# Two extra f16 products per group of heads in the causal self-attention of a three-layer kernel

## The reference, cut to what matters

```python
def _L0_attn_ref(x, Wq, bq, Wk, bk, Wv, bv, Wo, bo):
    B, S, E = x.shape                      # 4, 128, 1024
    H = 16; D = E // H                     # 16 heads of 64
    q, k, v = ...                          # three projections, rope on q and k
    scores = jnp.einsum('bshd,bthd->bhst', q, k) / jnp.sqrt(jnp.asarray(D, x.dtype))
    scores = jnp.where(causal[None, None], -jnp.inf, scores)
    attn = jax.nn.softmax(scores, axis=-1)
    out = jnp.einsum('bhst,bthd->bshd', attn, v).reshape(B, S, E)
    return out @ Wo + bo
```

## Time and profile before

| | us |
|---|---|
| median of 3 runs (lowest to highest) | 2761.11 (2759.78 to 2761.98) |
| the profiled execution, its own time | 2763.46 |
| its span, first to last instruction | 2761.6 |
| TensorE busy in the span | 2529.8 (92%) |
| VectorE / ScalarE / GpSimd busy | 2068.7 (75%) / 1142.1 (41%) / 859.8 (31%) |
| mean granted TensorE clock | 0.964 of 2.4 GHz |

### The profile page before, as it was taken

One profiled execution on the slowest core, in us unless ns is written; L12 is line 12 of the kernel. 1 busy time (PEld: TensorE's weight loads), 2 busy tenths in 40 slices (PEclk: granted clock), 3 DMA queues, 4 the chain that ended last, 5 costly groups with the idle time before them and its releaser, 6 DMA issues. The chain is left out here.

```text
span 2761.6 us, 42893 instructions
## 1 busy us (share of the span) xinstructions
PE 2529.8 (92%) x16296; PEld 1286.5 (47%) x16296; DVE 2068.7 (75%) x2971; ACT 1142.1 (41%) x1096; POOL 859.8 (31%) x381
## 2 busy tenths in 40 slices
PE   6999999999999999999778888888868999999998
PEld 3444444444444444444344545545444458444443
DVE  7788778777877778777689999999965434766664
ACT  3322222222222222222489999999982124311100
POOL 0232222322232222321455646556521460111100
PEclk9999999999999999999799999999988995899999
DMA  6134433444344433444568888888863222000000
GB/s 252 48 89 122 122 99 94 119 122 106 93 112 122 122 97 94 120 122 103 149 169 195 202 211 187 196 210 189 201 176 117 102 74 55 1 16 16 1 4 31
DMA packets 557343, 321.54 MB, mean 116 GB/s; under 512 B 401968, under 2 KB 533296, under 8 KB 552368
## 3 DMA queue, kind: packets, MB, share of 16 engines
q1 hardware_dynamic: 557232, 319.91, 45.0%
HBM read 149.95 MB, written 69.21 MB: 79 GB/s over the span
## 5 line engine op out<-in xcount | busy, mean ns | idle before, releaser
L1253 DVE TENSOR_SCALAR_CACHE_REDUCE at_sc<-at_score 128x1024 f32<-128x1024 f32 x512 | 601.6, 1219 | 22.5 <-PE at_score L1132 14.8
L1351 ACT ACTIVATE at_sc<-at_sc,at_bias,at_qs 128x4096 uint16<-128x4096 f32 x128 | 484.9, 3792 | 1.1 <-DVE at_bias L1265 1.1
L646 PE MATMUL kv_vacc<-kv_whi,kv_xthi 128*128 128x512 f16 x1024 | 388.8, 380 | 5.9 <-PEq L274 5.9
L646 PE MATMUL kv_vacc<-kv_wlo,kv_xthi 128*128 128x512 f16 x1024 | 388.7, 380 | 0.0
L646 PE MATMUL kv_vacc<-kv_whi,kv_xtlo 128*128 128x512 f16 x1024 | 388.6, 379 | 0.0
L654 PE MATMUL kv_kacc<-kv_wk,q_t 128*128 128x512 f16 x1536 | 348.7, 380 | 5.8 <-DVE kv_key L799 5.8
L725 ACT ACTIVATE q_t<-q_t 128x512 f16<-128x512 f32 x128 | 77.1, 626 | 505.7 <-POOL q_t L909 332.7
L907 POOL TENSOR_TENSOR q_t<-kv_rows 128x512 f32<-128x512 f32 x32 | 41.4, 1295 | 701.2 <-DMA kv_rows<-in_ctx 614.4
L654 PEld LDWEIGHTS kv_kacc<-kv_wk,q_t 128*128 128x128 f16 x1536 | 150.5, 98 | 188.6 <-issue 8.7
L731 ACT ACTIVATE o<-kv_key 128x1024 f16<-128x1024 f32 x64 | 67.7, 1057 | 397.7 <-DVE kv_key L818 397.7
L654 PE MATMUL kv_kacc<-kv_wk,kv_xthi 128*128 128x512 f16 x768 | 228.4, 379 | 0.7 <-DVE kv_xtlo L503 0.7
(11 more groups left out here) (230 smaller groups left out, 4243.5 us busy)
## 6 DMA issues: line engine op xcount, KB each, us to landing
kv_rows<-in_ctx SPq DMA_DIRECT2D x64, 512.0 KB, 6.9
values<-kv_val SPq DMA_DIRECT2D x32, 1024.0 KB, 6.4
keys_turned<-o SPq DMA_DIRECT2D x32, 1024.0 KB, 5.1
at_v_raw<-values SPq DMA_DIRECT2D x16, 2048.0 KB, 8.4
at_kt<-keys_turned SPq DMA_DIRECT2D x32, 512.0 KB, 5.2
x<-keys_turned SPq DMA_DIRECT2D x31, 512.0 KB, 5.1
x<-in_x SPq DMA_DIRECT2D x2, 2048.0 KB, 8.6
kv_wk<-in_wq SPq DMA_DIRECT2D x2, 2048.0 KB, 13.0
```

Of the source, the lines that this page charges most:

```text
L646: last = nc.tensor.matmul(v_acc[2 * s + c][:], a[s][:, k, :], b[:, c, k, :], start=(k == 0 and q == 0), stop=(k == KD - 1 and q == 2))
L1253: nc.vector.tensor_scalar(sc[n % 2][:, c * SC:(c + 1) * SC], score[pos % 2][:], 1.0, None, ALU.mult, ALU.max, accum_out=part_max[n % 2][:, ...
L1351: nc.scalar.activation(prob[n % 2][e], sc[n % 2][:, e * EC:(e + 1) * EC], ACT.Exp, bias=bias[n % 2][:], scale=qs_pair[j][:, t:t + 1], accu ...
```

## The change

A seventh PSUM bank, `spare`, is allotted for the block. A function `keep_busy` issues one f16 product of 128x128 weights by 128x512 columns, both taken from the high part of panel 8, into that bank; no instruction reads it and the call has no wait. It is called twice for each group: between scores(g+1) and turns(g), and between turns(g) and sums(g-1). That is 32 more weight loads and 32 more matmuls. No other engine's list changes.

```diff
         outp = [chip.ps(ctx, f"ca_outp{n}", [P, HG, P], F32) for n in range(2)]
+        spare = chip.ps(ctx, "ca_spare", [P, HALF], F32)
+        wide = panels.parts[split - 1][0]
         block = ctx.enter_context(nc.Block())
@@
+            def keep_busy():
+                nc.tensor.matmul(spare[:], wide[:, 0, 0:P], wide[:, 0, :], start=True, stop=True)
+
             def sums(g):
@@
             for g in range(G):
                 if g + 1 < G:
                     scores(g + 1)
+                keep_busy()
                 turns(g)
+                keep_busy()
                 if g >= 1:
                     sums(g - 1)
             sums(G - 1)
```

## The result

The changed kernel took 2769.19 us (median of 9 runs, 2767.47 to 2769.81), the kernel before 2761.73 (9 runs). The ratio is 1.0026, 95% interval 1.0016 to 1.0036: slower by 7.5 us, where 9.5 was forecast. The profiled execution took 2767.47 us, the shortest of the nine, with a span of 2765.7.

A forecast was written before the change was run, and what follows sets the result against it. Before the change, TensorE's own work and the path through ScalarE were taken as nearly equal bounds. Period terms summed to 9.9 us, taken as 9.5, on 2761.1: 2770.6 us, own range 2768 to 2774, 8-in-10 range 2753 to 2775.

The forecast's parts named there:

- TensorE alone is the bound: Attention block's periods after the change: TensorE's own work sets the 5.50 us period, with ScalarE's path hidden behind it.
- 0.77 per period: Eleven ordinary periods: two products at 0.43 us each, less 0.09 us of slack, lengthen each; 8.5 us in all.
- the slack of 0.09: Ordinary period before the change: 4.73 us against TensorE's own work of 4.64 us leaves this many us.
- the step from 9.9 to 9.5: Reduction of the summed us, because transposes' weights can load beside the product ahead of them, some 0.05 us each period.
- The single periods: Periods outside the ordinary: first + 0.86 us, ScalarE's panel half 0, VectorE's panel half - 0.35, last + 0.43.
- Behind the last transposes: End of the block, ahead of sums(14) and sums(15): one added product costs + 0.43 us.
- The clock stays at 0.50: Attention block: too little gapless full-height work, 1.8 us per period, to bring the clock back; chance 0.60.
- It will still fall at the start, since one product fills a twelfth: Block start: one 0.22 us product in the 2.63 us wait for ScalarE doesn't keep the clock from falling.
- Rival A: Block's clock returns early and holds, since time at work counts, not rows; period 3.6 us, 2743 us; chance 0.12.
- Rival B: Clock returns for part of the block, falling again in the panel periods; 2757 us, between 2750 and 2765; chance 0.18.
- Rival C: Products largely hidden by larger slack, only the one behind the transposes counts; 2767 us at most, perhaps 2765; chance 0.10.

The follow-up runs named there:

- the kernel with two and two: Changed kernel with two full-height products instead of one at each of the two places per group, 64 in all; 2755.17 us, ratio 0.9978.

## Why the prediction was right

The sign, the size and the mechanism held, but for one term.

**TensorE alone is the bound** held: ScalarE waits for the reciprocal, and the transposes wait for nobody in ordinary groups. **0.77 per period** was 0.70. The price of the product behind the transposes, 0.43, and the slack of 0.09 were as read; what the prediction named as given back by the weight load, some 0.05 a period, was 0.07. Over eleven periods that is 0.8 us; the step from 9.9 to 9.5 took off 0.4, though its own 0.05 would have been 0.6 or more.

**The single periods** were within 0.13 us each.

**Behind the last transposes** is the term that was mis-sized: + 0.43 foreseen, - 1.02 in the profiled execution. The clock came up at 2349.2, when product, transposes, product and sums had followed each other with no half-height scores between them, the last scores being done. The kernels with one product have no such rise and 5.62 and 6.05 us there. Nor has the kernel with only the start filled, whose last groups are the changed kernel's: 6.05 us, the + 0.43 that was foreseen. So the rise doesn't follow from these instructions alone, and the prediction could not have read it from them; what tips it is open. How many executions of the changed kernel have it isn't known; its runs spread over 2.3 us. By its own signs the prediction had ruled out any 1.00 in the block; these 3.4 us are the exception.

**The clock stays at 0.50** held for 78 of the block's 89 us, and the experiments bear out the reason given. The prediction set the height of the work against its time with nothing but the kernel's own rises to go by. Five kernels now say the same: with equal counts of products 2755 against 2784 us and 2744 against 2783, and full-height scores alone bring it back. That the sums stream 64 columns behind a load of 128 may count as well was argued in the prediction, and wasn't tried.

**It will still fall at the start, since one product fills a twelfth** held: the transposes still waited 2.31 us of 2.63. The kernel that filled that wait kept the clock until the next long one.

**Rival A** was wrong for this change and right as a sum: where the clock did hold, the time was 2744, for which the prediction had 2743, with a period of 3.72 us for the 3.6 worked out. Its mechanism, that only time at work counts, is what the half-height runs refute. **Rival B** describes the kernel with two and two: lost behind a panel half, 2755, and the one with the start filled, 2761. **Rival C** falls, since the second product alone costs 5.7 us and the first 3.8.

The Trainium skill, "TensorE: Matmul & The Clock Gate", section "Why this matters for your kernels", advises to keep TensorE busy. The runs agree only in part: 88.89 of 90.00 us busy, with half-height products in it, stayed at 0.50.

## What to carry to other kernels

Where a stretch of small products shows a granted clock of 0.50, look at the rows they use before adding work: half-height products don't count like full ones, and added work that doesn't bring the clock back only costs its price at 1.2 GHz. If it is to be tried, put full-height products into the long waits, and enough in every round to hold the clock; here 56 of them turned + 7.5 us into - 17.7. They are free in a wait only while the clock is up: at 0.50 seven and ten of them made the panel periods 2.1 and 2.7 us longer. Judge it by the granted clock of the stretch, because the sign of the change turns on it.

## What the runs showed of the hardware that was not expected

Two products on different halves of the rows ran side by side: periods of 5.98 and 6.77 us in turn, by whether scores and added products shared a half. And one and the same work kept the clock where it was, at either level: with one product on each side of the transposes, 52.59 of 64.80 us busy stayed at 1.00 where the long waits were filled, and 77.90 of 78.40 us in the changed kernel stayed at 0.50. In these kernels the clock was cheaper to keep than to get back: the start of the block, where it is still up, was the place to spend the first products.
